# Graph transformer layer on one core: the message pass with its routing work cut into parts and its row sends moved

## What is computed

```python
xn = _layernorm(x, axis=-1)
x = x + gnn(xn, src, dst, ...) + mix(xn[None], ...)[0]
x = x + ffn(_layernorm(x, axis=-1)[None], ...)[0]

# gnn: a softmax weight per edge, then the weighted source rows summed by destination
msg = feature[src] * alpha[:, None]
agg = jax.ops.segment_sum(msg, dst, num_segments=n)

# ffn: top-1 routing by softmax, place in the expert by a running count, capacity C
idx = jnp.argmax(probs, axis=-1)
pos = (jnp.cumsum(one_hot, axis=0) * one_hot).sum(-1).astype(jnp.int32) - 1
kept = pos < C
buf = jnp.zeros((E, C, D)).at[idx, jnp.where(kept, pos, C)].set(x, mode='drop')
y_tok = ybuf[idx, jnp.minimum(pos, C - 1)] * (prb * kept)[:, None]
```

## Time and profile before

| | us |
|---|---|
| median of 3 runs | 2648.24 |
| lowest and highest of them | 2640.82, 2654.11 |
| span of the profiled execution, first to last instruction | 2181.3 |
| median less span | 466.9 |
| in the span: projections and scores | 0 to 1201.8 |
| message pass | 1201.8 to 1757.3 |
| experts | 1757.3 to 2181.3 |

### The profile page before, as it was taken

One profiled execution on the slowest core, in us unless ns is written; L12 is line 12 of the kernel. 1 busy time (PEld: TensorE's weight loads), 2 busy tenths in 40 slices (PEclk: granted clock), 3 DMA queues, 4 the chain that ended last, 5 costly groups with the idle time before them and its releaser, 6 DMA issues. The chain is left out here.

```text
span 2181.3 us, 44890 instructions
## 1 busy us (share of the span) xinstructions
PE 1899.4 (87%) x12055; PEld 1346.6 (62%) x12055; DVE 1486.4 (68%) x6582; ACT 781.6 (36%) x3785; POOL 1223.5 (56%) x1251
## 2 busy tenths in 40 slices
PE   8997888878888888888887899999999679999997
PEld 5654555545555545555544566666666479999996
DVE  7775788878887888788787587666767624343433
ACT  6772444444444444444443011111111123333332
POOL 0006777777777777777774576656766312222222
PEclk9997889889888899899898799889999789999998
DMA  7867888888888888888885898877978566565650
GB/s 238 245 220 208 254 243 253 248 242 242 254 245 241 251 247 250 241 253 250 246 253 165 249 313 264 266 234 254 323 245 259 157 242 200 195 202 191 204 186 28
DMA packets 287974, 507.17 MB, mean 233 GB/s; under 512 B 59024, under 2 KB 199730, under 8 KB 287580
## 3 DMA queue, kind: packets, MB, share of 16 engines
q1 hardware_dynamic: 212556, 279.91, 40.8%
q0 software_dynamic: 75152, 224.23, 34.3%
HBM read 394.78 MB, written 112.83 MB: 233 GB/s over the span
## 5 line engine op out<-in xcount | busy, mean ns | idle before, releaser
L836 POOL DMA_INDIRECT pool_mem<-node_tab,edges x592 | 580.9, 981 | 346.1 <-issue 339.7
L1659 POOL DMA_INDIRECT main<-node_tab,edges x294 | 287.6, 978 | 189.2 <-issue 81.6
L967 PE MATMUL psum<-main 32*128 32x258 f32 x1568 | 217.3, 468 | 76.9 <-DVE main L1088 73.6
L977 PE MATMUL psum<-pool_mem,ident 128*128 128x258 f32 x592 | 201.0, 469 | 34.4 <-DMA pool_mem<-node_tab,edges 34.3
L876 ACT ACTIVATE main<-score_all,neg_max 128x8 f32<-128x8 f32 x98 | 29.6, 302 | 555.0 <-DVE neg_max L1119 555.0
L836 POOL DMA_INDIRECT main<-node_tab,edges x192 | 189.5, 987 | 58.5 <-issue 54.2
L2655 POOL DMA_INDIRECT out_dram<-pool_mem x56 | 56.9, 1016 | 282.3 <-DVE pool_mem L2752 266.6
L2685 PEld LDWEIGHTS psum<-pool_mem,main 128*128 128x128 f32 x1792 | 210.9, 194 | 3.3 <-issue 0.5
L2685 PE MATMUL psum<-pool_mem,main 128*128 128x128 f32 x1792 | 211.3, 277 | 0.1
L1000 PE MATMUL psum<-wkvT,main 128*128 128x512 f32 x392 | 200.6, 637 | 7.8 <-ACT main L886 7.5
L882 ACT ACTIVATE main<-main 128x64 f32<-128x64 f32 x784 | 197.9, 334 | 24.1 <-DVE main L1133 23.6
(11 more groups left out here) (284 smaller groups left out, 3656.8 us busy)
## 6 DMA issues: line engine op xcount, KB each, us to landing
main<-in_L_ffn_w_dram SPq DMA_DIRECT2D x64, 1024.0 KB, 5.4
main<-kept_rows SPq DMA_DIRECT2D x98, 640.0 KB
kept_rows<-pool_mem SPq DMA_DIRECT2D x74, 640.0 KB, 5.5
kept_rows<-main SPq DMA_DIRECT2D x24, 640.0 KB
node_tab<-pool_mem SPq DMA_DIRECT2D x49, 258.0 KB, 3.0
main<-proj_t SPq DMA_DIRECT2D x392, 32.2 KB
pool_mem<-node_tab,edges POOLq DMA_INDIRECT x592
moe_in<-zeros SPq DMA_DIRECT2D x32, 258.0 KB, 3.8
```

Source lines behind the costliest of these rows:

```text
L836: g.indirect_dma_start(source_rows(r, u, ZW + D), None, node_tab, bass.IndirectOffsetOnAxis(ap=edges[:, 0, HALF * k + u:HALF * k + u + 1], ...
L967: mm = pe.matmul(psum[:, Z_BANK[q], 0:ZW], hot_T[h][rows_q, j * P:(j + 1) * P], t_win[rows_q, h, :], start=True, stop=(pair in BY_VECTOR), ...
L977: pe.matmul(psum[:, Z_BANK[u % GROUPS_W], 0:ZW], ident[:, :], source_rows(r, u, ZW), start=False, stop=True).then_inc(s_z, 1)
L1659: g.indirect_dma_start(rows_g[k % R3][:, u - KEEP, 0:n], None, node_tab, bass.IndirectOffsetOnAxis(ap=edges[:, 0, HALF * k + u:HALF * k + ...
```

## The change

- `spread` is cut into three parts a step over four steps for batches 0 to 2 (four over three steps for 3 and 5; six a step as before for 4, 6, 7), and the tiles' `normalise`, `turn`, `logit` begin correspondingly later (`TURN_AT` 5, 5, 5, 4, 3, 4, 3, 3 in place of 3).
- `route_choice` is in eight parts, four a step over two steps (all eight in one step for batches 6 and 7), at r = 16, 17 for batches 0 to 2, at 15, 16 for batch 3 and 14, 15 for batch 4. `rank` comes a step after the last part (r = 18, 17, 16) instead of in the same step; in batches 6 and 7 it stays in the same step.
- `route_slots` is in eight parts: two a step over r = 19 to 22 for batches 0 to 2, four a step over two steps for 3 and 4, all in one step for 5 to 7. Each part begins with `dve.wait`.
- the copies into the row slots are taken out of it (`address`). For batches 0 to 4 they run one tile at a time, in the step of that tile's `send`.
- `send` begins at r = 23 for batches 0 to 2 and at r = 20 for batch 3, one tile in every second step; at r = 19 for batch 4, one a step. So batch 1 sends in steps 51, 53 ... 63, batch 2 in 65 ... 77, batch 3 in 76, 78 ... 88, batch 4 in 89 to 95. Batch 5 sends in steps 99 to 104 (before: 98 to 103); 6 and 7 as before.
- `gate_b` and `token_b` get two buffers, since a batch's values are now read while the next one's are made.

No arithmetic is added or taken away.

```diff
+        TURN_AT = [5, 5, 5, 4, 3, 4, 3, 3]
+        SPREAD_PARTS = [3, 3, 3, 4, 6, 4, 6, 6]
+        LOGITS_AT = [TURN_AT[b] + SIZES[b] + 3 for b in range(BATCHES)]
+        CHOICE_AT = [SIZES[b] + (9, 9, 9, 8, 7, 8, 8, 8)[b] for b in range(BATCHES)]
+        CHOICE_PARTS = [4, 4, 4, 4, 4, 4, 8, 8]
+        RANK_AT = [SIZES[b] + (11, 11, 11, 10, 9, 10, 8, 8)[b] for b in range(BATCHES)]
+        SLOTS_AT = [SIZES[b] + (12, 12, 12, 11, 10, 11, 10, 10)[b] for b in range(BATCHES)]
+        SLOTS_PARTS = [2, 2, 2, 4, 4, 8, 8, 8]
+        SEND_AT = [SIZES[b] + (16, 16, 16, 13, 12, 11, 10, 10)[b] for b in range(BATCHES)]
+        SEND_EVERY = [2, 2, 2, 2, 1, 1, 1, 1]
+        ONE_BY_ONE = 5
...
-            return [STARTS[b] + k - 10 - SIZES[b] - 2 * STARTS[b + 1] for b in range(BATCHES) if 0 <= k - 10 - SIZES[b] - 2 * STARTS[b + 1] < SIZES[b]]
+            return [STARTS[b] + i for b in range(BATCHES) for i in range(SIZES[b]) if 2 * STARTS[b + 1] + SEND_AT[b] + SEND_EVERY[b] * i == k]
...
-                        for i in range(n):
-                            t = STARTS[b] + i
-                            wait(v, s_h, t + 1)
-                            v.tensor_copy(hrow[:, t % HR, D:D + 1].bitcast(I32), token_b[:, i:i + 1]).then_inc(s_rows_done, 1)
-                            v.tensor_copy(hrow[:, t % HR, D + 1:D + 2], gate_b[:, i:i + 1]).then_inc(s_rows_done, 1)
...
+                    def address(t):
+                        b = BATCH_OF[t]
+                        i = t - STARTS[b]
+                        wait(v, s_h, t + 1)
+                        v.tensor_copy(hrow[:, t % HR, D:D + 1].bitcast(I32), token_b[:, b % 2, i:i + 1]).then_inc(s_rows_done, 1)
+                        v.tensor_copy(hrow[:, t % HR, D + 1:D + 2], gate_b[:, b % 2, i:i + 1]).then_inc(s_rows_done, 1)
...
-                        for b in in_batch(k, 1):
-                            for n in range(6):
-                                spread(b, n)
-                        for b in in_batch(k, 2):
-                            for n in range(6, RSQRT_STEPS + 2):
-                                spread(b, n)
-                        for b in tiled(k, 10):
-                            route_slots(b)
-                        for b in tiled(k, 6):
+                        for b in range(BATCHES):
+                            for part in parts_at(k, b, 1, SPREAD_PARTS[b], RSQRT_STEPS + 2):
+                                spread(b, part)
+                            for part in parts_at(k, b, SLOTS_AT[b], SLOTS_PARTS[b], 8):
+                                route_slots(b, part)
+                            if k == 2 * STARTS[b + 1] + SLOTS_AT[b] and b >= ONE_BY_ONE:
+                                for t in range(STARTS[b], STARTS[b + 1]):
+                                    address(t)
+                        for t in sent_at(k):
+                            if BATCH_OF[t] < ONE_BY_ONE:
+                                address(t)
+                        for b in batch_at(k, LOGITS_AT):
                             route_logits(b)
-                        for b in tiled(k, 8):
-                            route_choice(b)
+                        for b in range(BATCHES):
+                            for part in parts_at(k, b, CHOICE_AT[b], CHOICE_PARTS[b], 8):
+                                route_choice(b, part)
```

More of the change, by code:

```diff
@@ L1425, in graph_transformer_kernel @@
         kept_b = m.take(G)
-        gate_b = m.take(G)
+        gate_b = m.take(2, G)
         trash_b = m.take(G)
-        token_b = m.take(G)
+        token_b = m.take(2, G)
         valid = m.take(1)
@@ L1449, in looked_up, with batch_at, parts_at, tile_at @@
             return HALF if k < EARLY else KEEP
-        def in_batch(k, offset):
-            return [b for b in range(BATCHES) if 2 * STARTS[b + 1] + offset == k]
-        def tiled(k, offset):
-            return [b for b in range(BATCHES) if 2 * STARTS[b + 1] + SIZES[b] + offset == k]
-        def tile_at(k, offset):
-            return [STARTS[b] + k - offset - 2 * STARTS[b + 1] for b in range(BATCHES) if 0 <= k - offset - 2 * STARTS[b + 1] < SIZES[b]]
+        def batch_at(k, steps):
+            return [b for b in range(BATCHES) if 2 * STARTS[b + 1] + steps[b] == k]
+        def parts_at(k, b, first, parts, n):
+            i = k - 2 * STARTS[b + 1] - first
+            return range(i * parts, min(n, (i + 1) * parts)) if i >= 0 else range(0)
+        def tile_at(k, steps, behind=0):
+            return [STARTS[b] + i for b in range(BATCHES) for i in range(SIZES[b]) if 2 * STARTS[b + 1] + steps[b] + behind + i == k]
         def sent_at(k):
-            return [STARTS[b] + k - 10 - SIZES[b] - 2 * STARTS[b + 1] for b in range(BATCHES) if 0 <= k - 10 - SIZES[b] - 2 * STARTS[b + 1] < SIZES[b]]
+            return [STARTS[b] + i for b in range(BATCHES) for i in range(SIZES[b]) if 2 * STARTS[b + 1] + SEND_AT[b] + SEND_EVERY[b] * i == k]
         def batch_logits(b):
@@ L2093, in route_logits, with route_choice @@
                         v.tensor_tensor(logits_n, logits_n, wide(red_n), ALU.subtract).then_inc(s_r, 1)
[L2095 removed]
+                    def route_choice(b, part):
                         n = SIZES[b]
                         expos_n, chosen_n, tmp_n, red_n, prob_n, expert_n = expos[:, 0:n, :], chosen[:, 0:n, :], tmp[:, 0:n, :], red[:, 0:n], prob[:, 0:n], expert[:, 0:n]
[L2098 to L2106 removed]
+                        if part == 0:
+                            wait(v, s_re, b + 1)
+                        dve.wait()
+                        if part == 0:
+                            dve.done(v.tensor_reduce(red_n, expos_n, AX.X, ALU.add))
+                        elif part == 1:
+                            dve.done(v.reciprocal(red_n, red_n))
+                        elif part == 2:
+                            dve.done(v.tensor_tensor(expos_n, expos_n, wide(red_n), ALU.mult))
+                        elif part == 3:
+                            dve.done(v.tensor_reduce(prob_n, expos_n, AX.X, ALU.max))
+                        elif part == 4:
+                            dve.done(v.tensor_tensor(tmp_n, expos_n, wide(prob_n), ALU.not_equal))
+                        elif part == 5:
+                            dve.done(v.scalar_tensor_tensor(out=tmp_n, in0=tmp_n, scalar=float(NE), in1=ids(n), op0=ALU.mult, op1=ALU.add))
+                        elif part == 6:
+                            dve.done(v.tensor_reduce(expert_n, tmp_n, AX.X, ALU.min))
+                        elif b == 0:
                             dve.then(v.tensor_tensor(chosen_n, wide(expert_n), ids(n), ALU.is_equal))
@@ L2112, in route_choice, with route_slots @@
                             v.tensor_tensor(chosen_n, wide(expert_n), ids(n), ALU.is_equal).then_inc(s_r, 1)
[L2114 removed]
+                    def route_slots(b, part):
                         n = SIZES[b]
[L2116 to L2141 removed]
```

73 lines of the change are left out of this document (36 added, 37 removed).

## The result

The changed kernel takes 2619.07 us (median of 4 runs, 2614.04 to 2625.33) against 2651.06 (4 runs, 2640.82 to 2654.11) for the kernel before: a ratio of 0.9869 with a 95% interval of 0.9823 to 0.9915, 32 us gained. The forecast was 2612.

A forecast was written before the change was run, and what follows sets the result against it. PE bounds the plain step, and POOL needs as much: 62.8 + 2.2 + 1.5 = 66.5 us a period. Four periods save 33.9, steps 85 to 96 save 2.6, the tail 0: 2648.2 - 36.5 = 2612 us, range 2594 to 2634.

The forecast's parts named there:

- The base: Whole run: 466.9 us between the 2181.3 us span and the 2648.24 us median, taken as outside the trace and unchanged.
- The wait at `rank`: PE's 2.07 us stand for the choice ahead of `rank` goes; `rank` itself then takes 1.9 us.
- The period: Fourteen steps of the message pass: 62.8 us of POOL work, plus 2.2 and 1.5, make 66.5 us.
- DVE's 2.2 us over at r = 2, 3: In that pair of a batch's steps DVE needs 10.3 us against 8.07, with no cover: 2.2 us a period.
- Nine sends in the fourth period: Steps 71 to 84 hold nine sends in place of seven: 2 x 1.3 us, paid out of the coupling.
- a coupling of 1.5: Loss a period from PE and POOL both being full, bounded between 0 and some 6 us, taken as 1.5.
- my term (b): A send waits for DVE's copies: nothing, except batch 3's first row counting on batch 2's last, 0 to 4.6 us, taken as 1.
- The tail: Behind step 97: batch 5's rank leaves the path, its slots and copies join it; -3 to +3 us, taken as 0.
- the gathers: Rival: POOL's gathers bound the message pass, DVE waits for rows, coupling is 6 us, a period 71.0; 2630 us, chance 0.16.
- the row slots: Rival: ACT's `normalise` waits for row slots once POOL lags PE, ten steps lost, 58 us; 2670 us, chance 0.07.
- the lock on POOL: Rival: gathers grow by the routing's 8.6 us of DVE time, a period 71.4; 2632 us, chance 0.05.
- My own sign for POOL: POOL's waits for PE's window sums (line 1831) in the stage were to fall from 73.1 to under 35 us.

The follow-up runs named there:

- experiment 5: The kernel before with one edit: `rank` of batches 0 to 5 one step later, in the step after the choice; ratio 0.9927 to the kernel before.
- experiment 6: The changed kernel with `rank` of batches 0 to 5 back in the step of the choice's last part; ratio 0.9894 to the kernel before.
- experiment 8: The changed kernel with nine of the twelve parts of `spread` left out; ratio 0.9890 to the kernel before.
- 4: The changed kernel with spread in two blocks of six, choice and slots in one block each, at the same first steps; ratio 0.9915 to the kernel before.
- experiment 9: The changed kernel with 96 more PE instructions in step 1, each a wait on a semaphore already at its value; ratio 0.9938 to the kernel before.
- Experiment 7: The changed kernel with batch 3 sending one row a step from step 78, and every batch's spread ahead of all slots; ratio 0.9875 to the kernel before.
- 12: On top of experiment 10, batches 0 to 2: logits a step earlier, choice over three steps, rank, slots and sends a step later; ratio 0.9853 to the kernel before.
- experiment 3: The changed kernel with rows sent one in every step in all batches, from the same first steps; ratio 0.9874 to the kernel before.
- experiment 10: The changed kernel with one row sent a step, and batch 5 as in the kernel before except its choice a step earlier; ratio 0.9873 to the kernel before.
- experiment 11: The kernel before with ten matmuls of zeros on PE ahead of `rank` of batches 0 to 5, in place of idle waiting; ratio 1.0010 to the kernel before.
- e2_after: The changed kernel run and profiled once more, no edit; ratio 0.9891 to the kernel before.
- e1_before: The kernel before run and profiled once more, no edit; 2648.87 us in its profile, ratio 1.0008.

## Why the prediction was right, and where its steps failed

The time fell as forecast, inside the range, and what the change was to remove, the wait at `rank`, is gone. That the size came out too is in part luck: the four periods were to give 10.2, 8.4, 6.9 and 8.4 us and gave 16.8, 8.9, 10.5 and -7.7, and the tail took back what steps 85 to 96 gave. The steps one by one:

- **The base.** "466.9 us lie outside what the trace shows; I carry them over unchanged" is wrong: 1.8 us lie outside. The Trainium skill, page "Runtime: NRT & Kernel Launch", section "The ~15µs preamble/postamble breakdown", puts the gap between a profile's total time and the reported one at about 6 us, whatever the kernel, the profile's being the longer. No run here shows that figure, since the span counts only from the first instruction to the last, and it lies 1.8 us below the time; but next to a gap of that size 467 us should have been read as a profile of an unlike execution. The forecast survived because it was a difference: 36.5 us against 28.3 in the stage by one pair of profiles and 33.6 by the other, and 27 to 32 in the medians.
- **The wait at `rank`.** Right: 14.6 us to 0.0, and experiment 5, which moves `rank` alone, shows it to be the main term. That moving it alone would bring more than half of the gain, and that it need not move once the choice is divided (experiment 6), was not foreseen.
- **The period.** Forecast 66.5, measured 71.9 to 92.9. The plain step was right to the digit: four take 16.15 us. What failed is the sum with a PE "at a granted clock of 0.97 or more": it is 0.95, 0.96, 0.92 and 0.84, and PE is busy 67 to 78 us a period in place of 62.4. Steps 85 to 96 take 63.8 in place of 56.3. The saving came out near the forecast (28.5 and 36.2 against 33.9) since both kernels stand above their sums.
- **DVE's 2.2 us over at r = 2, 3.** The sign I set for myself has come: steps 44 and 45 take 12.1 us (1834.85 to 1846.94), over 11. But experiment 8 takes DVE's work away there and gains nothing that can be measured, so the term was mis-sized: about 0 in place of 2.2, while PE still stands ahead of that look-up (2.67 us in step 44, below). It stands for DVE's `lows`, and DVE is late there mostly from before its routing: in step 43 it stands 3.00 us for a look-up that PE's records end at 1828.72, 2.6 us before DVE is released, and 1.09 us more behind that, while its routing and copies ahead of the next `alphas` take 1.2 us (1836.23 to 1837.47). Why that release comes late stays open (last section).

```profile
1827.40 1.32 PE L1866 MATMUL psum<-tab_sum,pool_mem 128*128 128x49 f32 x10 [0.44 <-issue]
...
1831.31 0.27 DVE L2036 SCALAR_TENSOR_TENSOR pool_mem<-count,attr,psum 128x49 f32<-128x49 f32 x1 [3.00 <-remote]
...
1836.23 0.17 DVE L2081 TENSOR_SCALAR pool_mem<-pool_mem 128x7 f32<-128x7 f32 x1
...
1837.09 0.21 DVE L2104 TENSOR_REDUCE pool_mem<-pool_mem 128x7 f32<-128x56 f32 x1
...
1839.42 1.32 PE L1866 MATMUL psum<-tab_sum,pool_mem 128*128 128x49 f32 x10 [2.67 <-DVE pool_mem L2020]
```

- **Nine sends in the fourth period,** put at 2 x 1.3 inside a coupling of 1.5. That period lost 3 to 8 us instead of gaining 8. It takes 87 to 96 us in the six profiles with nine spaced sends in it (both of the change, 4, 6, 8, 9) and 90.2 with eleven (7), but 86.1 with nine that are not spaced (12), 80.6 and 85.3 with eight (3, 10), 82 to 85 with seven (the kernel before, 5, 11). Experiment 7 speaks against the counted order, my term (b). That it is the sends is argued from these, not shown, and a rival fits as well: two of the stalls of the last section, in steps 71 and 79, lie in this period. These two steps take 9.9 and 10.7 us in `e2_after` and 3.3 and 6.5 in experiment 3 on the same chip: 10.8 us, more than the 7.9 between the two periods. No run parts the two causes. It is no loss as a whole, as experiment 3 has the same time without it.
- **The tail.** Taken as 0 (-3 to +3), measured +5.3 and +4.8 against the 43.4 of `e1_before`. That one profile is at the low end: experiment 11, with the same order behind step 97, has 46.4. On one chip each, batch 5 in its old place gives 44.6 (12) against 48.2 (`e2_after`), and 43.7 (10) against 48.0 (9), so the term is rather +4. The step that failed is "the two are of like size": I let batch 5's `rank` drop out of the path, and it only moved along it. DVE in the changed kernel between the last tile's measure (L2076) and batch 7's first spread part (L2081), with PE's rank:

```profile
2154.54 0.18 DVE L2076 BATCH_NORM_AGGREGATE pool_mem<-pool_mem 128x2 f32<-128x6 f32 x1
2154.67 0.40 PE L1898 MATMUL psum<-pool_mem,above 128*128 128x48 f32 x2
...
2156.80 0.21 DVE L2144 TENSOR_TENSOR pool_mem<-psum,pool_mem 128x48 f32<-128x48 f32 x1 [2.07 <-PE psum L1902]
...
2159.89 0.16 DVE L2081 TENSOR_SCALAR pool_mem<-pool_mem 128x3 f32<-128x3 f32 x1
```

DVE stands 2.07 us for rank and then spends 3.1 on slots and copies: 5.35 us from measure to spread, where experiment 10, which puts batch 5 back, takes 0.22:

```profile
2109.43 0.18 DVE L2076 BATCH_NORM_AGGREGATE pool_mem<-pool_mem 128x2 f32<-128x6 f32 x1
2109.65 0.17 DVE L2081 TENSOR_SCALAR pool_mem<-pool_mem 128x3 f32<-128x3 f32 x1
```

- **The rivals.** None took over. Groups on POOL, DVE and ACT in the changed kernel's stage (gathers; DVE's first instruction behind gathered rows; `normalise`):

```profile
L1671 POOL DMA_INDIRECT main<-node_tab,edges x294 | 283.1, 963 | 263.4 <-PE psum L1843 81.8 <-issue 63.1 <-remote 56.8
```

```profile
L2033 DVE TENSOR_TENSOR pool_mem<-main,score_all 128x3 f32<-128x3 f32 x94 | 14.6, 155 | 4.7 <-DMA main<-node_tab,edges 3.0 <-issue 1.7
```

```profile
L1753 ACT ACTIVATE pool_mem<-pool_mem 128x256 f32<-128x256 f32 x49 | 29.5, 602 | 9.6 <-DVE pool_mem L2087 5.3 <-issue 4.3
```

DVE waits 3.0 us for gathered rows, not 50 (3.7 in the like profile of the kernel before, where the earlier trace rows has 34.7): the gathers do not bound, and the coupling of 1.5 us a period is not seen in this wait. `normalise` waits for no send: the row slots are wide enough. A gather takes 963 ns, as in the like profile of the kernel before. The prediction took the lock on POOL from the Trainium skill's page "SBUF — State Buffer", section "SBUF: two separate sides", by which GpSimd cannot write descriptors while a DVE copy in a two-port mode holds their shared ports; it is not seen here either. My own sign for POOL failed, 81.8 us of standing for PE's window sums instead of under 35, as PE's periods did not shrink to POOL's 62.8; it was 119.0 in the like profile of the kernel before.

## What to carry to other kernels

When one engine's long insertion meets another engine's consumer in the same step, first try to move the consumer by a step: here that one edit brought some 0.6 of the gain, and dividing everything else added 0.4 to 0.6% of the time, no more than the intervals are wide. Look at the end of the pipeline by itself: a step's delay of a batch in the middle cost nothing that can be seen here, and at the end it landed on the path, with some 4 us. Before any sum, hold the profile's span against the timed runs: here a gap of hundreds of us meant that the profile shows another kind of execution.

## What the runs showed of the hardware

The same program ran in two ways: the first profile of the kernel before has no idle time put down to "issue" ahead of a window sum or a look-up in these periods, while its second profile has 15.7 us ahead of the look-up alone, and the other kernels' have 5.6 to 14.6. A plain step is the same in both, 16.13 and 16.15 us for four, but in each later profile steps 5-8, steps 9-12 or both take longer, 17 to 23 us. The two ways differ in when DVE is released to read a look-up's results. In the first profile it never starts more than 0.6 us after the look-up's recorded end while it stands for nothing else; in every later profile it does so in 24 to 37 of the 98 steps, for 48 to 77 us in all (55 in `e1_before`, whose message pass is 74 us longer than in the first profile). What ended DVE's waits ahead of these readings, in us, times and longest, in the first profile (the only line) and in `e1_before` (two of three):

```profile
DVE pool_mem L2024 <- PE psum L1854: 70.1, 63, 4.6
```

```profile
DVE pool_mem L2024 <- PE psum L1854: 83.9, 46, 5.1
DVE pool_mem L2024 <- remote: 42.8, 12, 7.3
```

"Remote" is a release that the profile cannot put beside the end of any instruction. PE's recorded ends are modelled, so whether PE ended later than recorded or its signal came late is not shown. PE's matmuls stand in some of these steps too. One such stall, in step 66 of `e2_after`:

```profile
1963.51 1.32 PE L1866 MATMUL psum<-tab_sum,pool_mem 128*128 128x49 f32 x10
...
1966.36 0.63 PE L1843 MATMUL psum<-main,pool_mem 128*32 128x256 f32 x7
...
1967.25 0.66 PE L1843 MATMUL psum<-main,pool_mem 128*32 128x256 f32 x5 [0.26 <-issue]
...
1968.73 1.10 PE L1843 MATMUL psum<-main,pool_mem 128*32 128x256 f32 x4 [0.83 <-issue]
...
1971.63 0.27 DVE L2036 SCALAR_TENSOR_TENSOR pool_mem<-count,attr,psum 128x49 f32<-128x49 f32 x1 [6.64 <-remote]
...
1973.51 2.37 PE L1866 MATMUL psum<-tab_sum,pool_mem 128*128 128x49 f32 x10 [3.67 <-DVE pool_mem L2020]
```

Sixteen matmuls with no wait among them, 1.07 us where undisturbed (as in this step of experiment 9), come in pieces. DVE needs none of them: it waits for the look-up that PE issued ahead of them, whose records end at 1964.83, and starts 6.8 us after that, 1.8 us after the modelled end of the last piece (1969.83). The next look-up then runs at the lower clock (granted 0.50, that is 1.2 GHz), 2.37 us against 1.32. In four profiles with the same order of PE's instructions (both of the change, experiments 4 and 8) the stalls stand in steps 66, 71 and 79; 96 instructions more moved one of them and left two. But experiments 3 and 7 have that order of PE's instructions too and differ in when rows are sent (7 also in the order of DVE's work): 7 has no stall in step 79 (6.6 us) and one in 83 (10.8), and 3 has none in 66, 71 or 79 (5.4, 3.3 and 6.5 us). So their place does not hang on PE's instructions alone. Nothing traced accounts for them, and their cause is open.
